# Second block of a two-layer cross-attention kernel: which engine begins the loads of the heads' keys, and the order of the transfer queue

## What is computed

```python
x = layer_norm(hidden_states, ln1_w, ln1_b)
q = (x @ q_w + q_b).reshape(B, LQ, H, HD)       # H = 16 heads, HD = 32
k = (context @ k_w + k_b).reshape(B, LK, H, HD)
v = (context @ v_w + v_b).reshape(B, LK, H, HD)
scores = einsum(q, k) / sqrt(HD), masked
out = softmax(scores) @ v
hidden = out @ cproj_w + cproj_b + hidden_states
y = hidden + mlp(layer_norm(hidden))
```

## Time and profile before

| | |
|---|---|
| median of 3 runs | 2245.2 us (2244.7 to 2251.22) |
| the profiled execution | 2248.41 us |
| its span, first to last instruction | 2246.6 us |
| attention of the second block, s = 0 to 31 | about 1781 to 2081 us of the span |
| instructions | 36949 |

### The profile page before, as it was taken

How to read it: one execution, slowest core, us unless ns; L and a number is a source line. 1 busy time by engine, 2 the same in 40 slices (tenths; PEclk the granted TensorE clock), 3 DMA queues, 4 the chain that set the end, 5 groups by cost and what they waited for, 6 DMA issues and landing times.

```text
span 2246.6 us, 36949 instructions
## 1 busy us (share of the span) xinstructions
PE 2161.7 (96%) x12468; PEld 2099.6 (93%) x12468; DVE 1560.9 (69%) x3631; ACT 1247.9 (56%) x2956; POOL 820.2 (37%) x754
## 2 busy tenths in 40 slices
PE   7999999999999999999999999999999889897999
PEld 6999999999999999999999999998999878786999
DVE  7777788777778877777887777787445477678341
ACT  5555555555555655555555555556356476567464
POOL 4313444242344424234442423442566311022255
PEclk9999999999999999999999999999999999999999
DMA  4657455565744555464555546454453656664243
GB/s 139 171 136 178 100 115 102 124 151 137 177 101 113 103 126 123 85 149 101 114 102 125 123 86 149 101 114 82 132 156 112 178 158 181 171 170 130 73 124 112
DMA packets 161447, 287.77 MB, mean 128 GB/s; under 512 B 35312, under 2 KB 92784, under 8 KB 161264
## 3 DMA queue, kind: packets, MB, share of 16 engines
q1 hardware_dynamic: 161264, 285.41, 53.2%
HBM read 240.32 MB, written 28.64 MB: 120 GB/s over the span
## 4 chain that ended last, share of the span: by engine, by line
PE 81%; DMA 5%; DVE 4%; ACT 3%; POOL 3%; issue 2%; SPq 2%; ACTq 0%; POOLq 0%; DVEq 0%
PE bank L871 77%; PE bank L964 3%; DMA ctxN_raw<-in_ctx 1%; POOL mring L806 1%; DMA k<-k_parts 1%; PE bank L1144 1%; DMA q_parts<-qs 1%; SPq L676 1%; PE bank L1133 1%; POOL mring L804 1%; DMA stage<-in_fb 1%; POOL ln_c L847 1%; DVE ln_c L1604 1%; DMA k_parts<-kT 0%; SPq L665 0%
## 5 line engine op out<-in xcount | busy, mean ns | idle before, releaser
L871 PE MATMUL bank<-ctxT,kring 128*128 128x362 f32 x3456 | 633.3, 331 | 5.5 <-DVE kT L1551 4.4
L871 PEld LDWEIGHTS bank<-ctxT,kring 128*128 128x128 f32 x3456 | 590.5, 191 | 8.4 <-issue 6.6
L806 POOL TENSOR_TENSOR mring<-stage,mring 128x512 fp32r<-128x512 f32 x325 | 442.4, 1367 | 165.6 <-ACT mring L1273 148.3
L871 PE MATMUL bank<-pT,ctxN 128*128 128x400 f32 (+1 forms) x2304 | 469.9, 351 | 0.7 <-DVE U L1555 0.4
L804 POOL TENSOR_SCALAR mring<-stage 128x512 fp32r<-128x512 f32 x205 | 144.1, 703 | 871.7 <-PE bank L871 718.8
L871 PEld LDWEIGHTS bank<-pT,ctxN 128*128 128x128 f32 (+1 forms) x2304 | 407.1, 188 | 2.5 <-issue 1.3
L871 PE MATMUL bank<-hT,mring 128*128 128x400 f32 x1608 | 320.9, 349 | 9.6 <-POOL mring L806 6.3
L871 PE MATMUL bank<-U,mring 128*128 128x400 f32 x1536 | 303.3, 348 | 8.1 <-issue 6.4
L871 PEld LDWEIGHTS bank<-hT,mring 128*128 128x128 f32 x1608 | 295.4, 190 | 15.9 <-POOL mring L806 9.2
L871 PEld LDWEIGHTS bank<-U,mring 128*128 128x128 f32 x1536 | 275.3, 188 | 10.4 <-issue 7.9
L1273 ACT ACTIVATE kT<-bank,cols 128x361 fp32r<-128x361 f32 (+1 forms) x288 | 160.7, 558 | 212.5 <-PE bank L871 212.4
(11 more groups left out here) (103 smaller groups left out, 2956.6 us busy)
## 6 DMA issues: line engine op xcount, KB each, us to landing
ctxN_raw<-in_ctx SPq DMA_DIRECT2D x256, 192.0 KB, 3.7
ctxT_raw<-in_ctx SPq DMA_DIRECT2D x64, 724.0 KB, 7.9
k<-k_parts SPq DMA_DIRECT2D x96, 181.0 KB, 3.4
stage<-in_wk SPq DMA_DIRECT2D x64, 256.0 KB, 4.9
stage<-in_wq SPq DMA_DIRECT2D x64, 256.0 KB, 4.3
stage<-in_wv SPq DMA_DIRECT2D x64, 256.0 KB, 4.2
stage<-in_wo SPq DMA_DIRECT2D x64, 256.0 KB, 2.7
stage<-in_fa SPq DMA_DIRECT2D x64, 256.0 KB, 2.6
```

What stands on the lines that cost most here:

```text
L806: nc.gpsimd.tensor_tensor(lo, src, f32(hi), ALU.subtract).then_inc(S.w_ready, 1)
L871: mm = pe.matmul(dst, parts_l[a], parts_r[b], start=first and k == 0, stop=last and k == len(order) - 1)
```

## The change

`load_k` moves from SP's queue to ACT's, with its waits. ACT begins step s + 1's keys right behind the exponential of step s's first head, u = 4s; `load_k(0)` stands behind `query1_high(3)`. On SP, save_q moves to the front of a step, load_q from s % 4 == 3 to s % 4 == 2 (for the first batch of the second half, NB = 4, to the end of step 14, behind move_heads), and load_ctxT from the middle of a step to its end, behind move_heads. In MLP step F = 30 ACT's high part of tile ("b", 31) now comes ahead of `key1_high(0)`. No arithmetic changes; PE's, DVE's and POOL's lists are the same.

```diff
             save_q(0)
             save_k(1)
-            load_k(0)
             save_q(1)
...
             for s in range(NS + BEHIND):
-                if s + 1 < NS:
-                    load_k(s + 1)
+                if s - 1 - S_Q1 in range(4):
+                    save_q(4 + s - 1 - S_Q1)
                 if s + AHEAD - 1 < NS:
                     save_k(s + AHEAD - 1)
-                if s % 4 == 1 and s // 4 + 2 < BATCH:
-                    load_ctxT(4 * GN + s // 4 + 2)
+                if s % 4 == 2 and s // 4 + 1 in range(2, BATCH) and s // 4 + 1 != NB:
+                    load_q(s // 4 + 1)
                 if s % 4 == 2 and s // 4 + 2 < BATCH:
                     load_mask(s // 4 + 2)
-                if s - 1 - S_Q1 in range(4):
-                    save_q(4 + s - 1 - S_Q1)
-                if s % 4 == 3 and s // 4 + 1 in range(2, BATCH):
-                    load_q(s // 4 + 1)
                 load_jobs(jobs_due(T_ATT1 + s - 1) + STAGE)
                 if s >= BEHIND:
                     move_heads(s - BEHIND)
+                if s == 4 * NB - 2:
+                    load_q(NB)
+                if s % 4 == 1 and s // 4 + 2 < BATCH:
+                    load_ctxT(4 * GN + s // 4 + 2)
...
+            def load_k(s):
+
+                act.wait_ge(S.k1_out[s % 2], 16 * (s // 2 + 1))
+                if s >= 2:
+                    act.wait_ge(S.s1_mm, HG * (s - 2) + HG)
+                else:
+                    act.wait_ge(S.o_mm, DC * GN)
+                for k, _, k_part in PARTS3:
+                    act.dma_start(f32(k3[k * HD1:(k + 1) * HD1, s % 2]),
+                                 k_dram[s, :, k_part].rearrange("(i r) n -> r i n", i=HG)).then_inc(S.k3_in[s % 2], 16)
...
                     elif m == 0 and F == NF - 2:
+                        tile_high(("b", NF * m + F + 1))
                         key1_high(0)
                     elif m == 0:
                         query1_high(0)
-                    if F + 1 < NF:
+                    if F + 1 < NF and not (m == 0 and F == NF - 2):
                         tile_high(("b", NF * m + F + 1))
...
             for Q in (1, 2, 3):
                 query1_high(Q)
+            load_k(0)
             values1_high(0, 0)
...
                     if u < NU1:
                         exponent1(u)
+                    if i == 0 and s + 1 < NS:
+                        load_k(s + 1)
```

More of the change, by code:

```diff
@@ L655, in save_k @@
                 sp.dma_start(k_dram[s], f32(kT[:, s % 2])).then_inc(S.k1_out[s % 2], 16)
[L657 to L666, removed]
             def move_heads(t):
```

## The result

The changed kernel takes 2258.36 us, median of 7 runs (2253.66 to 2261.47), against 2250.14 us for the kernel before in the same comparison: a ratio of 1.0035, 95% interval 1.0024 to 1.0046. It is slower by 8 us, a third of a percent, and outside the predicted range. Its profiled execution took 2253.66 us at a span of 2251.9 us, against 2246.6 before.

A forecast was written before the change was run, and what follows sets the result against it. It took PE as busiest in a chain with DVE and ACT, idle 36.5 of 300 us in attention. Gains of 27 us less 14 us for ACT's begins made 13, so 2245.2 would become 2232 us, range 2216 to 2250.

The forecast's parts named there:

- (a): Attention, first heads of batches: loading queries a step earlier removes PE's waits for load_q; 10 us gained, bounds 7 to 12.
- (b): Attention, save of query 6: begun 2 us earlier, it lands before ACT wants it; the whole 4.6 us wait goes.
- What is late next: Attention: once query waits go, the softmax chain is late next, so 10 us was taken of 11.9.
- Handed on: Rival, chance 0.19: the softmax chain's waits grow by what load_q's waits lose; about 1 us of gain, 2244 us.
- (c): MLP tile ("b", 31) written earlier: 2.0 us off PE's 2.35 us wait, plus 1 us at the attention's start.
- (d): Attention, key loads begun by ACT: keys land sooner and 3 us of PE's 4.7 us waits go, bounds 0 to 4.7.
- the keys are there 6.0 to 6.6 us into a step: Attention: key landing time reckoned from a begin 1.1 to 1.7 us into a step, against steps of 7.0 to 8.5.
- (e): TensorE's clock recovers where waits go: 1.7 us for (c) and about 5 us for the rest, bounds 2 to 10.
- ACT's begins: Attention: three DMA instructions a step on ACT delay the work behind them; cost 14 us, bounds nothing to 53.
- The criterion: PE's waits for pT and ACT's scaling together: near 15 us the ACT term is wrong, above 30 too small.
- Hidden: Rival, chance 0.18: ACT's DMA instructions cost next to nothing, hidden in its idle time; 2219 us.
- ACT bound: Rival, chance 0.15: SP's head moves hold ACT's begins, 2.9 us a step; attention lasts 320 us, kernel 2261 us.

The follow-up runs named there:

- e4: The kernel before with only load_q and save_q moved as in the change, keys still begun by SP: 2233.8 us, ratio 0.9918.
- e1: The kernel before with only the MLP edit, the high part of tile b 31 ahead of key1_high(0): 2249.9 us, ratio 0.9994.
- e3: The changed kernel with only the context load put back to its old place in the middle of a step: 2248.4 us, ratio 0.9985.
- e8: The kernel before with the change's whole order of SP's queue, late context load included, but keys kept on SP: 2245.1 us, ratio 0.9973.
- e12: The changed kernel with the context load mid-step and the three key begins spread, one behind each of three exponentials: 2256.0 us, ratio 1.0029.

## Why the prediction was wrong, point by point

- **What bounds the kernel, (a) and (b): right.** The waits at steps 8, 16, 24 and 28 and ACT's wait for q_parts are gone. With their share of the clock I had 14.6 us and up to 5; e4 measures 17, of which 13 for the loads. "What is late next" took nothing: the waits for pT and scaling stayed at 14.6 us. So the rival Handed on was wrong.
- **(c), the tile: the mechanism right, the gain not kept.** The POOL wait fell below 0.5 us as predicted, but e1 is unchanged. One step that failed is the sentence that took away PE's first wait of the attention as well, because three key transfers leave SP's queue ahead of `load_q(0)`: begun by ACT, they run beside the last save that `load_q(0)` waits for, it comes only 1.2 us sooner, and the wait grew from 0.80 to 2.27 us. What takes the rest of the gain in e1 is open. I counted 4.7 us with the clock; e1 puts it between a gain of 4.5 and a loss of 1.8 us, around 1.
- **(d), loads of keys: the wrong sign, the first of the two large errors.** This step failed: "the keys are there 6.0 to 6.6 us into a step". I reckoned 4.9 us from first begin to last landing (1.5 and the 3.4 of the earlier trace rows), a median, and no spread. The median was 4.7 us before and 5.7 in the changed kernel, and for the six groups nearest to a context load it was 6.2 to 10.3 us. Instead of 3 us less, the waits for keys grew by 8.6; without the late context load they are at e3's 8.4, 3.7 more than before and no gain on e4's 8.9. On one queue step 2's keys stood ahead of the first context load (begun at 1786.7 and 1789.8); on two the context load was begun first (1785.4, keys 1787.0), and the wait of 5.2 us followed. Nor are the steps of the earlier trace rows typical: from step 0 to 31 the kernel before needs 292.25 / 31 = 9.4 us a step, not 7.0 to 8.5. The rule of the Trainium skill that I weighed, "DMA: Bandwidth & Descriptors", section "Issuing engines are not separate DMA queues", came nearer with its 0: the same DMA engines carry everything.
- **The late context load: passed over in one sentence.** "load_ctxT comes one step later and has three steps to spare" asked only when the context is needed, not what it stands in front of, and so put the cost at nothing. e3 and e8 show 10 and 11 us for this move alone. This is the largest single thing that the sum left out.
- **(e), the clock: right in e4, not in the changed kernel.** e4's PE needs 3.5 us less for the same work, within my 2 to 10. In the changed kernel new waits replaced the old ones and it needs 3.1 us more.
- **ACT's begins: the size right.** Predicted 14 us; between e4 and e3 it is 15. That the two agree so well is in part luck: the 15 also hold the longer first wait, the tile, and PE's slower work (258.5 against 253.6 us). The criterion, pT and scaling together between 15 and 30, gave 21.8. I found most of the damage where I had looked for it, in the steps with s % 4 == 1 (7.0 us more of waits for pT in e3 than in e4, against my 9.8), though it reached PE as waits for the values' low part as well, and in other steps. The rival Hidden was wrong, except for the first begin of each three. The rival ACT bound forecast 2261 and a slower kernel, near the measurement, but by luck: ACT needs 1.3 us a step for its begins and not 2.9, and is busy 195 us of 303.

In sum I forecast -13 us and measured +8. (a), (b), (e) 19.6 against 17 or 18; (c) 4.7 against about 0; (d) and the context load 3 against -11; ACT's begins -14 against -15. The differences are 2, 5, 14 and 1 us, 22 in sum, against the 21 between forecast and measurement. The forecast time, 2232, is another 5 us off, since it starts from 2245.2 and the seven runs of the kernel before have their median at 2250.14.

## What to carry over

Ask of a transfer that is moved not only when its own data is needed but which urgent transfer is begun in the microseconds behind it, on any engine's queue: a load of 1.4 MB one place ahead of a load that is wanted at the next step cost 10 us here, and a queue of its own didn't help. A compute engine can begin a transfer for nothing while its datapath is at work, but only so many as fit beside the running instruction; here one, not three. Before a second engine is brought in, try the order of the one queue, which gave 22 us here, 17 of them for the queries alone.

## What the runs showed of the hardware

- Beginning transfers on ACT costs by what exceeds the running instruction: three begins of 1.8 us behind an exponential of 0.79 us left ACT idle 1.16 us, one of 0.51 us left it idle 0 us.
- The begin of a 181 KB key load on ACT took 0.31 to 0.46 us in 63 of 96 cases of the changed kernel, and 1.47 us at the longest; three in a row took 1.33 us by median and up to 2.55 us. Of e12's, spread, 73 of 96 took 0.31 to 0.32 us.
- The landing of one and the same 181 KB transfer went from 2.6 us to 9.3 us in the changed kernel, the longest beside a context load of 1.4 MB begun by another engine 1.6 us earlier.
- The last save of queries (two transfers of 200 KB) was followed by the load that waits for it after 3.4 to 3.8 us in the nine kernels with the keys on SP, and after 5.5 to 5.7 us in the five where ACT had begun step 0's keys just ahead of it.
- The same three begins of 1.8 us a step cost 18 us behind a step's first exponential and 7.5 behind its last. I haven't shown by a run which instruction makes the difference; the rows point to the values tile that follows the first.
